# Experts of a small language-model tower: VectorE's small operations dealt out one by one, `up` moved behind `down`, side work moved to other steps

## Chip, cores and metric

One core of a Trainium2 chip. The time is device microseconds of the whole program; the kernel before takes 2905.35 us (median of 3 runs, 2901.58 to 2911.56).

## What is computed

4096 tokens of width 192 pass through an embedding with a block-wise quantisation, an attention layer of 12 heads, and a layer of experts. Only the last is touched:

```python
z = jnp.einsum('nd,sdr->nsr', xf, P)            # xf: layer norm of h; 8 sets, 16 numbers each
scores = jnp.einsum('nsr,smr->nsm', z, C)       # 64 experts in each set
topv, topi = jax.lax.top_k(scores, K)           # K = 4
w = jax.nn.softmax(topv, axis=-1)
h = jax.nn.gelu(jnp.einsum('nsr,nskrh->nskh', z, W1g) + b1g)   # 32 hidden units
yl = jnp.einsum('nskh,nskhr->nskr', h, W2g) + b2g
comb = jnp.einsum('nskr,nsk->nsr', yl, w).reshape(n, S * R)
out = jax.nn.gelu(comb @ G1 + g1b) @ G2 + g2b   # h + out is the result
```

## The kernel before

The experts' stage (`stage_experts`) computes all 64 experts of each set for all tokens, and multiplies the hidden values by a weight that is zero for those not chosen. Tokens go in 8 groups of 512 (NG, GTOK). A group has 32 steps (NSTEP), each with four blocks of 128 hidden rows. A block's way: `up` (L1340) multiplies z by W1 into one of the four PSUM banks 0 to 3; ScalarE's `gelu` (L1483) takes two banks (a pair, 0 or 1) at once into `hid`; `spread_weights` (L1353) copies the block's weights over its rows into one of three ring banks; VectorE's mixture, `mix` (L1609, recorded at L1615), multiplies the two into `hw`; `down` (L1360) adds four blocks by W2 into bank 7, four matrix products on four column groups, in two recorded passes each. `up` reads 50 rows of one half of the array's rows, `spread` 64; z and the weights lie so that each `up` stands on the other half than the `spread` beside it.

TensorE's order in step n is written out by hand: `spread` 2 of step n, the first `up` of pair 1 for step n+1, `down` of step n-1, `spread` 3, the second `up` of that pair, `spread` 0 of step n+1, the first `up` of pair 0 for n+2, `spread` 1, the second `up`; then side items. Each engine runs its own list in order. The first `up` of a pair waits for the GELU that reads its banks (L1342); `down` for the four mixtures of its step.

The three ring banks (`order`, `at`, `ring_bank`, `bank_free`) are dealt out in one list over all `spread` and side items: an item waits until the third one before it has been read. `sides` names the side items of each step: `OUT_AT` the way out of the group before (mixture of sets, GELU, product, `take_out` on VectorE in steps 3 and 4, then GpSimd adds the input in `add_input` and SP stores); `PREP_AT` the scores of the next group (items 3 to 6, two banks at a time) and the turnings of its weights (items 7 to 10); `Z_AT` the turnings of x and `make_z` (items 0 to 2) for the group after the next.

VectorE's own small work for later groups stands between mixtures, in bursts: `normalise` (layer norm) behind the second mixture of steps 7, 13 and 15, `prepare` (maxima, marks, denominators, `keep_marked`, `high_weights`) behind the fourth of steps 14 to 25, `split_z` behind step 22. Eight maxima or marks make a burst. On GpSimd `weights` (L1267) runs `below_best`, `divide` for both halves and then `low_weights` for both halves; `turn_w` (L1329) waits for `low_weights` of its half. ScalarE computes `exponentials` behind step 18.

z goes through HBM and back (`bounce_z`, L1194). SP's list per group g is: `bounce_z(g + 1)`, wait for the output of group g, store it. `score` (L1316) waits for z (`z_in`).

Of the kernel before, what the change touches and what calls it, by code (L numbers as in the profile page):

```python
# [15 lines left out]
ALU = mybir.AluOpType  # L16
# [7 lines left out]
GT = 4  # L24
NG = NT // GT
# [5 lines left out]
S, R, M, HID = 8, 16, 64, 32  # L31
NJ = M * HID // P
NQ = 4
# [902 lines left out]
def stage_experts(nc, f_p, f_c, f_w1, f_b1, f_w2, f_b2, f_g1, f_g1b, f_g2, f_g2b,  # L936
# [15 lines left out]
    TAKEN = -3.0e38  # L952
    NSTEP = 2 * NJ
# [5 lines left out]
    with ExitStack() as own:  # L959
# [26 lines left out]
        side_full, side_free, out_taken = sem("side_full"), sem("side_free"), sem("out_taken")  # L986
# [10 lines left out]
        def work(n):  # L997


            pair, jj = divmod(n, NJ)  # L1000
            return [(2 * pair + i // 2 + NQ * (i % 2), (jj + NJ // 2 * (i % 2)) % NJ) for i in range(4)]
# [140 lines left out]

        Z_AT = {16: (0,), 17: (1,), 20: (2,)}
        PREP_AT = {12: (3, 4), 14: (5, 6), 26: (7,), 27: (8,), 28: (9,), 29: (10,)}
        OUT_AT = {1: (0,), 2: (1,), 3: (2,)}
        EXP_AT = 18
        SPLIT_AT = 22
        BIAS_AT = (18, 21)  # L1150

        def sides(g, n):
            found = [("out", g - 1, k) for k in OUT_AT.get(n, ())] if g else []
# [28 lines left out]
        def ring_bank(item):  # L1182
            return psum[FIRST + at[item] % RING]
# [36 lines left out]
        def _(pool):  # L1220
# [22 lines left out]

            def divide(g, part):
                half = slice(part * GT * S // 2, (part + 1) * GT * S // 2)
                pool.wait_ge(marked, 2 * g + part + 1)
                pool.tensor_tensor(ew[:, half, :], ew[:, half, :],
                                   rden[:, 1, half].unsqueeze(2).to_broadcast([P, GT * S // 2, M]), ALU.mult)\
                    .then_inc(w_scaled, 1)
# [37 lines left out]
        def _(pe):  # L1287
# [49 lines left out]
                                            ident16[:, :])  # L1337
                last.then_inc(side_full, 1)

            def up(g, n, pair, which):  # L1340
                if which == 0:
                    need(pe, gelu_done, g * (2 * NSTEP) + 2 * n - 1 + pair)  # L1342

                low_rows = work(n)[2 * pair][1] < NJ // 2
                i = 2 * pair + (which + 1 if low_rows else which) % 2
                s, j = work(n)[i]
                rows = slice(HALF * (s // NQ), HALF * (s // NQ) + KR)
                last = pe.matmul(psum[i], w1[rows, s % NQ, j * P:(j + 1) * P], zst[rows, g % 2, s % NQ, :],  # L1348
                                 start=True, stop=True)
                if which:  # L1350
                    last.then_inc(up_done, 1)
# [56 lines left out]
            for item in FIRST_ITEMS:  # L1408
                side(*item)
            pe.wait_ge(w_copied, 4)  # L1410
            for n, pair in ((0, 0), (0, 1), (1, 0)):
                up(0, n, pair, 0)
                up(0, n, pair, 1)
            for i in (0, 1):
                spread_weights(0, 0, i)
            for g in range(NG):
                for n in range(NSTEP):
                    next1, next2 = after(g, n), after(g, n, 2)
                    last1 = after(g, n, -1)
                    spread_weights(g, n, 2)  # L1420
                    if next1[0] < NG:
                        up(*next1, 1, 0)
                    if g or n:
                        down(*last1)
                    spread_weights(g, n, 3)
                    if next1[0] < NG:
                        up(*next1, 1, 1)
                        if next1[1] == 0:
                            pe.wait_ge(w_copied, next1[0] * 4 + 4)
                        spread_weights(*next1, 0)  # L1430
                    if next2[0] < NG:
                        up(*next2, 0, 0)
                    if next1[0] < NG:
                        spread_weights(*next1, 1)
                    if next2[0] < NG:
                        up(*next2, 0, 1)
                    if n in BIAS_AT:
                        bias_down(g, BIAS_AT.index(n))
                    for item in sides(g, n):
                        side(*item)  # L1440
# [96 lines left out]
        def _(dve):  # L1537
# [20 lines left out]
            def refine(g):  # L1558
                dve.wait_ge(pow_done, g + 1)
                link(dve.tensor_tensor(newton, rstd, rstd, ALU.mult))  # L1560
                link(dve.tensor_tensor(newton, newton, var, ALU.mult))
                link(dve.tensor_scalar(newton, newton, -0.5, 1.5, ALU.mult, ALU.add))
                dve.tensor_tensor(rstd, rstd, newton, ALU.mult).then_inc(rstd_ready, 1)

            def split_z(g):
                dve.wait_ge(zh_done, g + 1)
                dve.wait_ge(side_free, freed_at["prep", g, 2])
                dve.tensor_tensor(zp[:, 1, :], zc[:, :], zp[:, 0, :].bitcast(F32), ALU.subtract)\  # L1568
                   .then_inc(z_split, 1)

            def top_four(g, k):
                t2, half = divmod(k, 2)
                dve.wait_ge(side_free, freed_at["prep", g, 3 + k])
                dve.memset(holder[:, k:k + 1], 0.0)
                for t in (2 * t2, 2 * t2 + 1):
                    for q in range(NQ):
                        i = (half * NQ + q) * GT + t
                        last = dve.max(top[:, i, :], sc[:, i, :])  # L1578
                if k == 3:
                    link(last)  # L1580

            def denominators(g):
# [1 line left out]
                                  top[:, :, TOPK:TOPK + 1].to_broadcast([P, GT * S, TOPK]), ALU.subtract)\  # L1584
                   .then_inc(den_asked, 1)

            def mark(g, part):
                for i in range(part * GT * S // 4, (part + 1) * GT * S // 4):
                    last = dve.match_replace(scr[:, i, :], top[:, i, :], sc[:, i, :], TAKEN)  # L1589
                if part == 3:  # L1590
                    link(last)

            def reciprocals(g):
# [2 lines left out]
                link(dve.reciprocal(rden[:, 1, :], rden[:, 0, :]))  # L1596

            def keep_marked(g, part):
                half = slice(part * GT * S // 2, (part + 1) * GT * S // 2)
                dve.scalar_tensor_tensor(ew[:, half, :], scr[:, half, 0:M], TAKEN, ew[:, half, :],  # L1600
                                         ALU.is_equal, ALU.mult).then_inc(marked, 1)

            def high_weights(g, part):
                half = slice(part * GT * S // 2, (part + 1) * GT * S // 2)
                by_half = ew[:, half, :].rearrange("p i (h m) -> p i h m", h=2)
                dve.wait_ge(w_scaled, 2 * g + part + 1)
                dve.tensor_copy(wsp[:, half, :, 0, :], by_half).then_inc(w_cast, 1)

            def mix(g, n, blocks):  # L1609
                if (g or n > 1) and 0 in blocks:  # L1610
                    dve.wait_ge(down_done, g * NSTEP + n - 1)
                for q in blocks:
                    dve.wait_ge(gelu_done, g * (2 * NSTEP) + 2 * n + q // 2 + 1)
                    dve.wait_ge(spread, g * (NQ * NSTEP) + NQ * n + q + 1)
                    dve.tensor_tensor(hw[:, n % 2, q, :], hid[:, n % 2, q, :], ring_bank(("w", g, n, q)),  # L1615
                                      ALU.mult).then_inc(mixed, 1)

            def take_out(g, k):
                if k == 0:
# [2 lines left out]
                dve.tensor_tensor(tok(o[:, :])[:, 2 * k:2 * k + 2, :],  # L1622
                                  ring_bank(("out", g, 1 + k)).rearrange("p (t n) -> p t n", t=2)[:, :, 0:D],
                                  g2b_bc[:, :].unsqueeze(1).to_broadcast([P, 2, D]), ALU.add).then_inc(out_taken, 1)
            def prepare(g, n):

                if 14 <= n < 18:
                    top_four(g, n - 14)
                if n == 17:
                    denominators(g)  # L1630
                if 18 <= n < 22:
                    mark(g, n - 18)
                if n == 22:
                    reciprocals(g)
                if n in (22, 23):
                    keep_marked(g, n - 22)
                if n in (24, 25):
                    high_weights(g, n - 24)

            def normalise(g, n):  # L1640

                if n == 7:
                    sums(g)
                if n == 13:
                    variance(g)
                if n == 15:
                    refine(g)

            for g in range(2):
                for n in range(NSTEP):  # L1650
                    normalise(g, n)
                split_z(g)
            for n in range(NSTEP):
                prepare(0, n)
            for g in range(NG):
                for n in range(NSTEP):
                    mix(g, n, (0, 1))
                    if g and n in (3, 4):
                        take_out(g - 1, n - 3)
                    if g < NG - 2:  # L1660
                        normalise(g + 2, n)
                    mix(g, n, (2, 3))
                    if g < NG - 1:
                        prepare(g + 1, n)
                    if n == SPLIT_AT and g < NG - 2:
                        split_z(g + 2)
            for k in range(2):
                take_out(NG - 1, k)

# [24 lines left out]
```

## Time and profile before

| | |
|---|---|
| median of 3 runs | 2905.35 us |
| the profiled execution | 2918.95 us, its span 2917.2 us |
| TensorE busy (matmul) | 2477.4 us, 85% |
| VectorE busy | 1895.8 us, 65% |
| ScalarE busy | 1200.4 us, 41% |
| GpSimd busy | 1155.5 us, 40% |
| mixtures, L1615 | 1024 of 683 ns |
| `up`, L1348; `spread`, L1358 | 1024 of 582 and of 421 ns |
| `down`, L1366 | 2048 records of 664 ns |

The experts run in the last third, from 1950 to the end. A view of the timeline gives for each line its start, its length, the engine, the source line, what it writes and reads, how many merged instructions, and in brackets how long the engine was idle before it and who released it. Matmuls on different parts of the array overlap, so their lengths don't add up. The granted clock is TensorE's, as a share of 2.4 GHz.

### The profile page before, as it was taken

How to read it: one execution, taken by the hardware profiler on the slowest of the kernel's cores; microseconds unless marked ns; L12 is line 12 of the kernel's file. 1: busy time of each engine (PE TensorE's matmuls, PEld its weight loads, DVE VectorE, ACT ScalarE, POOL GpSimd, SP SyncE). 2: the span in 40 equal slices, each digit the busy share in tenths (PEclk: the TensorE clock that was granted, in tenths of full speed). 3: DMA queues.
4: the chain of work that ended last, by engine and by line, in shares of the span. 5: the costliest groups of instructions: out<-in, count | busy, mean ns of one | idle time of the engine just before them, and what ended most of it. 6: DMA issues, size and time to landing. Idle time of an engine off the chain costs nothing. (4 is left out here: it accounts for less than half of the span.)

```text
span 2917.2 us, 42124 instructions
## 1 busy us (share of the span) xinstructions
PE 2477.4 (85%) x16000; PEld 1240.8 (43%) x16000; DVE 1895.8 (65%) x3858; ACT 1200.4 (41%) x1617; POOL 1155.5 (40%) x781
## 2 busy tenths in 40 slices
PE   3556999999999999999999996048888888888898
PEld 1223555565555556555555653022323323232232
DVE  5865565565655656565555654147878888788786
ACT  3421333333333333333333332035656666566565
POOL 5000475666757566575756654021120111201010
PEclk9788999999999999999999998558989999798899
DMA  1002000000010000000000002810101011010100
GB/s 45 11 22 55 7 1 9 1 9 9 1 30 1 9 1 9 9 1 9 1 2 1 3 1 10 72 36 1 24 1 24 1 24 24 1 24 1 24 6 6
DMA packets 78699, 38.51 MB, mean 13 GB/s; under 512 B 62937, under 2 KB 71193, under 8 KB 77849
## 3 DMA queue, kind: packets, MB, share of 16 engines
q1 hardware_dynamic: 76320, 30.98, 6.2%
q10 hardware_dynamic: 640, 1.69, 0.5%
q0 software_dynamic: 1536, 3.15, 0.4%
q8 instruction: 127, 2.08, 0.3%
q14 instruction: 76, 0.61, 0.1%
HBM read 21.93 MB, written 10.49 MB: 11 GB/s over the span
## 5 line engine op out<-in xcount | busy, mean ns | idle before, releaser
L588 POOL TENSOR_TENSOR acc<-acc,pT 128x1024 f32<-128x1024 f32 (+3 forms) x412 | 830.0, 2015 | 243.7 <-ACT pT L907 210.4
L1615 DVE TENSOR_TENSOR hw<-hid,banks 128x512 f32<-128x512 f32 x1024 | 645.7, 683 | 192.0 <-PE banks L1358 187.3
L907 ACT ACTIVATE pT<-banks 128x1024 f32<-128x1024 f32 x480 | 405.7, 896 | 831.1 <-PE banks L661 818.2
L787 DVE TENSOR_REDUCE part<-banks 128x2 f32<-128x1024 f32 (+3 forms) x432 | 438.3, 1044 | 311.7 <-PE banks L637 310.0
L1487 ACT ACTIVATE hid<-banks 128x1024 f32<-128x1024 f32 x512 | 499.5, 1022 | 333.3 <-PE banks L1348 314.7
L1348 PE MATMUL banks<-zst,w1c 50*128 50x512 f32 x1024 | 425.9, 582 | 29.2 <-ACT hid L1487 23.3
L1358 PE MATMUL banks<-wT,select 64*128 64x512 f16 x1024 | 357.5, 421 | 61.6 <-DVE hw L1615 56.9
L677 PE MATMUL banks<-pT,v 128*64 128x512 f32 (+3 forms) x1920 | 404.7, 542 | 1.5 <-POOL pT L576 1.5
L1366 PE MATMUL banks<-hw,w 128*32 128x512 f32 x2048 | 302.0, 664 | 1.4 <-DVE hw L1615 0.8
L1358 PEld LDWEIGHTS banks<-wT,select 64*128 64x128 f16 x1024 | 98.9, 98 | 439.9 <-DVE hw L1615 355.7
L637 PE MATMUL banks<-kh,qh 64*128 64x512 f32 (+1 forms) x960 | 191.1, 393 | 14.5 <-ACT pT L907 5.6
L677 PEld LDWEIGHTS banks<-pT,v 128*64 128x64 f32 x1920 | 116.6, 136 | 202.9 <-issue 180.1
L1348 PEld LDWEIGHTS banks<-zst,w1c 50*128 50x128 f32 x1024 | 169.5, 206 | 76.3 <-ACT hid L1487 68.7
L657 PE MATMUL banks<-shift_rows,ones 64*128 64x512 f32 x960 | 198.9, 411 | 0.2 <-DVE part L787 0.2
L637 PE MATMUL banks<-kl,qh 64*128 64x512 f32 (+1 forms) x960 | 176.3, 362 | 0.0
L637 PE MATMUL banks<-kh,ql 64*128 64x512 f32 (+1 forms) x960 | 176.2, 362 | 0.0
L576 POOL TENSOR_SCALAR_AFFINE_SELECT pT<-pT 128x256 f32<-128x256 f32 x192 | 78.1, 407 | 247.0 <-ACT pT L907 246.8
L661 PE MATMUL banks<-qh,kh 64*128 64x512 f32 x960 | 175.8, 362 | 0.0
L661 PE MATMUL banks<-ql,kh 64*128 64x512 f32 x960 | 175.3, 361 | 0.0
L661 PE MATMUL banks<-qh,kl 64*128 64x512 f32 x960 | 175.3, 361 | 0.0
L657 PEld LDWEIGHTS banks<-shift_rows,ones 64*128 64x128 f32 x960 | 89.8, 183 | 194.8 <-issue 131.2
L830 DVE RECIPROCAL total<-total 128x256 f32<-128x256 f32 x96 | 167.6, 1746 | 3.1 <-ACT total L915 2.7
(183 smaller groups left out, 2901.0 us busy)
## 6 DMA issues: line engine op xcount, KB each, us to landing
zst<-z_scratch SPq DMA_DIRECT2D x48, 128.0 KB, 4.4
z_scratch<-zp SPq DMA_DIRECT2D x8, 512.0 KB, 3.5
out_h<-o SPq DMA_DIRECT2D x8, 384.0 KB, 2.7
xT_scratch<-xs_hi SPq DMA_DIRECT2D x4, 512.0 KB, 2.7
xt_hi<-xT_scratch SPq DMA_DIRECT2D x2, 1024.0 KB, 5.6
w1c<-raw1p ACTq DMA_DIRECT2D x12, 132.0 KB, 4.6
w1c<-raw1p SPq DMA_DIRECT2D x12, 132.0 KB, 4.1
wo<-in_L_attn_W_O SPq DMA_DIRECT2D x12, 96.0 KB, 1.9
```

What stands on the lines that cost most here:

```text
L588: pool.tensor_tensor(acc[:, G % 2, :, off:CH], acc[:, G % 2, :, off:CH], pT[:, slot, :, 0:w], ALU.add).then_inc(summed, 1)
L637: last = pe.matmul(banks[h][:, 0:w], a[head(h), u, i * P:(i + 1) * P], b[head(h), u, c * CH:c * CH + w], start=(k == 0), stop=(k == 2))
L657: pe.matmul(banks[h][:, 0:w], ones[head(h), :], rows[head(h), u, Q, off:CH], start=True, stop=False)
L661: last = pe.matmul(banks[h][:, 0:w], a[head(h), u, kt * P:(kt + 1) * P], b[head(h), u, t0:t0 + w], start=False, stop=(k == 2))
L677: last = pe.matmul(psum[6 + G % 2][head(h), off:CH], v[:, u, kt, head(h)], pT[:, J % PSLOTS, h, 0:CH - off], start=(kt == 0), stop=(j == L ...
L787: last = dve.tensor_reduce(to[:, :, c:c + 1], both[:, :, 0:whole], AX.X, ALU.max)
L907: act.activation(pT[:, J % PSLOTS, :, 0:CH - off], both[:, :, 0:CH - off], ACT.Exp, scale=E ** -0.5)\
L1348: last = pe.matmul(psum[i], w1[rows, s % NQ, j * P:(j + 1) * P], zst[rows, g % 2, s % NQ, :], start=True, stop=True)
L1358: pe.matmul(bank, select[rows, jr, :], wT[rows, g % 2, s, :], start=True, stop=True).then_inc(spread, 1)
L1366: last = pe.matmul(psum[Y][32 * i:32 * i + 32, :], w2[:, s, j, :], hw[:, n % 2, i, :], start=(n == 0), stop=(n == NSTEP - 1))
L1487: act.activation(hid[:, n % 2, 2 * pair:2 * pair + 2, :], banks[:, pair * 1024:(pair + 1) * 1024].rearrange("p (q n) -> p q n", n=GTOK), A ...
L1615: dve.tensor_tensor(hw[:, n % 2, q, :], hid[:, n % 2, q, :], ring_bank(("w", g, n, q)), ALU.mult).then_inc(mixed, 1)
```

## The change

Everything is in the experts' stage. The arithmetic is the same.

- VectorE: one maximum behind each mixture of steps 8 to 15, one mark behind each of steps 16 to 23. `keep_marked` goes in quarters instead of halves (behind the third mixtures of steps 20 and 21, the first and the third of 24), `high_weights` behind the second mixtures of 23 and 26, denominators at 16, reciprocals at 20, sums, variance and refine behind the first mixtures of 5, 7 and 9, `split_z` behind the last of 15. `divide` waits for two quarters. A mark's or a maximum's last one still has VectorE wait for its end, now also at each eighth mark.
- TensorE: `spread` 2, `down`, `spread` 3, first `up` of pair 1, `spread` 0, second `up`, `spread` 1, then both `up` of pair 0. The pair's first product is chosen to lie on the other half of the rows than the `spread` before it.
- Side work: `Z_AT` from 16, 17, 20 to 11, 12, 13; the scores from 12 and 14 to 5 and 7; the turnings of the weights from 26 to 29 to 24, 25, 27, 28; exponentials from 18 to 17; biases from (18, 21) to (18, 22). SP's and GpSimd's lists stay.

```diff
-        Z_AT = {16: (0,), 17: (1,), 20: (2,)}
-        PREP_AT = {12: (3, 4), 14: (5, 6), 26: (7,), 27: (8,), 28: (9,), 29: (10,)}
+        Z_AT = {11: (0,), 12: (1,), 13: (2,)}
+        PREP_AT = {5: (3, 4), 7: (5, 6), 24: (7,), 25: (8,), 27: (9,), 28: (10,)}
         OUT_AT = {1: (0,), 2: (1,), 3: (2,)}
-        EXP_AT = 18
-        SPLIT_AT = 22
-        BIAS_AT = (18, 21)
+        EXP_AT = 17
+        BIAS_AT = (18, 22)
+        BEST_FROM, MARK_FROM = 8, 16
+        KEEP_AT = {(20, 2): 0, (21, 2): 1, (24, 0): 2, (24, 2): 3}
+        HIGH_AT = {(23, 1): 0, (26, 1): 1}
+        DEN_AT, RECIPROCALS_AT = (16, 0), (20, 0)
+        SUMS_AT, VARIANCE_AT, REFINE_AT, SPLIT_AT = (5, 0), (7, 0), (9, 0), (15, 3)
+        TAKE_OUT_AT = {(3, 1): 0, (4, 1): 1}
...
-                pool.wait_ge(marked, 2 * g + part + 1)
+                pool.wait_ge(marked, 4 * g + 2 * part + 2)
...
-            def up(g, n, pair, which):
+            def up(g, n, pair, which, beside=None):
                 if which == 0:
                     need(pe, gelu_done, g * (2 * NSTEP) + 2 * n - 1 + pair)
-
-                low_rows = work(n)[2 * pair][1] < NJ // 2
-                i = 2 * pair + (which + 1 if low_rows else which) % 2
+                    first_of[pair] = 2 * pair
+                    if beside is not None:
+                        gw, nw, iw = beside
+                        first_of[pair] += work(nw)[iw][1] < NJ // 2
+                i = first_of[pair] if which == 0 else 4 * pair + 1 - first_of[pair]
...
                     spread_weights(g, n, 2)
-                    if next1[0] < NG:
-                        up(*next1, 1, 0)
                     if g or n:
                         down(*last1)
                     spread_weights(g, n, 3)
                     if next1[0] < NG:
-                        up(*next1, 1, 1)
+                        up(*next1, 1, 0, (g, n, 3))
                         if next1[1] == 0:
                             pe.wait_ge(w_copied, next1[0] * 4 + 4)
                         spread_weights(*next1, 0)
-                    if next2[0] < NG:
-                        up(*next2, 0, 0)
-                    if next1[0] < NG:
+                        up(*next1, 1, 1)
                         spread_weights(*next1, 1)
                     if next2[0] < NG:
+                        up(*next2, 0, 0, (*next1, 1))
                         up(*next2, 0, 1)
...
-            def mark(g, part):
-                for i in range(part * GT * S // 4, (part + 1) * GT * S // 4):
-                    last = dve.match_replace(scr[:, i, :], top[:, i, :], sc[:, i, :], TAKEN)
-                if part == 3:
+            def mark(g, i):
+                last = dve.match_replace(scr[:, i, :], top[:, i, :], sc[:, i, :], TAKEN)
+                if i % (GT * S // 4) == GT * S // 4 - 1:
                     link(last)
...
             for g in range(NG):
-                for n in range(NSTEP):
-                    mix(g, n, (0, 1))
-                    if g and n in (3, 4):
-                        take_out(g - 1, n - 3)
+                for n, q in GAPS:
+                    mix(g, n, q)
+                    if g and (n, q) in TAKE_OUT_AT:
+                        take_out(g - 1, TAKE_OUT_AT[n, q])
                     if g < NG - 2:
-                        normalise(g + 2, n)
-                    mix(g, n, (2, 3))
+                        normalise(g + 2, n, q)
                     if g < NG - 1:
-                        prepare(g + 1, n)
-                    if n == SPLIT_AT and g < NG - 2:
-                        split_z(g + 2)
+                        choose(g + 1, n, q)
```

## Rows read from the trace of the kernel before

**Rows 1.** Busy time in windows (us), mixtures alone, then all engines, clock, DMA.
```profile
2086.70:2814.50 727.80, 485.26 (x769) 0.91 0.07 15
...
2821.20:2903.30 82.10, 73.28 (x446) 22.76 (x438) 65.79 (x106) 49.68 (x52) 0.00 (x0) 1.00 0.02 6
```

**Rows 2.** Timeline of a plain step: `up`, `down`, `spread`, the fourth mixture, GELUs.
```profile
2231.18 0.49 PE L1348 MATMUL banks<-zst,w1c 50*128 50x512 f32 x1
2231.60 1.07 PE L1366 MATMUL banks<-hw,w 128*32 128x512 f32 x8
...
2232.60 0.39 PE L1358 MATMUL banks<-wT,select 64*128 64x512 f16 x1
2232.60 0.61 PE L1348 MATMUL banks<-zst,w1c 50*128 50x512 f32 x2
...
2233.09 2.48 DVE L1615 TENSOR_TENSOR hw<-hid,banks 128x512 f32<-128x512 f32 x4 [0.60 <-PE banks L1358]
2233.20 1.94 ACT L1487 ACTIVATE hid<-banks 128x1024 f32<-128x1024 f32 x2 [1.15 <-PE banks L1348]
```

**Rows 3.** Group 2 by windows, mixtures alone: VectorE busy, clock, DMA share, GB/s.
```profile
2197.70:2211.10 13.40, 10.09 (x16) 1.00 0.01 2
2211.10:2220.60 9.50, 7.53 (x12) 1.00 0.29 102
2220.60:2233.05 12.45, 9.93 (x16) 1.00 0.44 61
2233.05:2294.50 61.45, 35.67 (x56) 0.87 0.00 1
2294.50:2316.90 22.40, 17.73 (x29) 0.97 0.00 1
```

**Rows 4.** Timeline of the last step: `spread` 2 with no `up` beside it, `down`.
```profile
2900.78 0.39 PE L1358 MATMUL banks<-wT,select 64*128 64x512 f16 x1 [0.51 <-DVE hw L1615]
2901.09 1.06 PE L1366 MATMUL banks<-hw,w 128*32 128x512 f32 x8
```

**Rows 5.** Timeline, VectorE: maxima in a burst; a mark.
```profile
2247.29 0.99 DVE L1578 MAX8 top<-sc 128x8 f32<-128x68 f32 x7
...
2267.11 0.21 DVE L1589 MATCH_REPLACE8 scr<-top,sc 128x68 f32<-128x68 f32 x1
```

**Rows 6.** Timeline, TensorE: scores; the first half of `make_z` at the full clock.
```profile
2240.66 1.08 PE L1325 MATMUL banks<-w1c,zst 48*128 48x64 f32 x16 [0.93 <-DVE hw L1615]
...
2518.07 1.13 PE L1313 MATMUL banks<-x2t_hi,pm_hi 128*128 128x512 f32 x2
```

**Rows 7.** Timeline in group 2: `take_out`, SP's issues; line L1204's landing.
```profile
2212.93 0.55 DVE L1622 TENSOR_TENSOR o<-banks,g2b_bc 128x384 f32<-128x384 f32 x1
...
2215.90 0.45 SPq L1198 DMA_DIRECT2D z_scratch<-zp  x1
2219.47 2.66 SPq L1204 DMA_DIRECT2D zst<-z_scratch  x6
...
DMA to landing us min/median/max: 2.9/4.4/5.8
```

**Rows 8.** Timeline, GpSimd: a half divided, a half's low parts.
```profile
2292.89 1.90 POOL L1247 TENSOR_TENSOR ew<-ew,rden 128x1024 f32<-128x1024 f32 x1 [1.84 <-DVE ew L1600]
...
2299.09 2.14 POOL L1255 TENSOR_TENSOR wsp<-ew,wsp 128x1024 f16<-128x1024 f32 x1 [1.05 <-DVE wsp L1607]
```

**Rows 9.** Timeline, ScalarE: first table load for the exponentials; GELUs after.
```profile
2268.56 1.28 ACT L1473 ACT_TABLE_LOAD   x1
...
2273.28 1.94 ACT L1487 ACTIVATE hid<-banks 128x1024 f32<-128x1024 f32 x2
```

**Rows 10.** Windows of group 2, all engines: an idle TensorE; the slow stretch behind.
```profile
2247.00:2249.00 2.00, 0.00 (x0) 0.01 (x1) 2.00 (x12) 1.57 (x2) 0.00 (x0) 1.00 0.00 0
...
2251.50:2258.30 6.80, 6.80 (x28) 2.54 (x25) 4.84 (x21) 3.07 (x4) 0.18 (x1) 0.50 0.01 2
```

**Rows 11.** Timeline, TensorE: `down` in that slow stretch.
```profile
2254.42 1.94 PE L1366 MATMUL banks<-hw,w 128*32 128x512 f32 x8
```

More of the change, by code:

```diff
@@ L1410, in _ @@
             pe.wait_ge(w_copied, 4)
+            first_of = [0, 0]
             for n, pair in ((0, 0), (0, 1), (1, 0)):
@@ L1569, in split_z, with best @@
                    .then_inc(z_split, 1)
-            def top_four(g, k):
+            def best(g, m):
+                k, r = divmod(m, GT * S // 4)
                 t2, half = divmod(k, 2)
[L1573 to L1579, printed above, removed]
+                if r == 0:
+                    dve.wait_ge(side_free, freed_at["prep", g, 3 + k])
+                    dve.memset(holder[:, k:k + 1], 0.0)
+                i = (half * NQ + r % NQ) * GT + 2 * t2 + r // NQ
+                last = dve.max(top[:, i, :], sc[:, i, :])
+                if m == GT * S - 1:
                     link(last)
@@ L1598, in keep_marked @@
             def keep_marked(g, part):
-                half = slice(part * GT * S // 2, (part + 1) * GT * S // 2)
-                dve.scalar_tensor_tensor(ew[:, half, :], scr[:, half, 0:M], TAKEN, ew[:, half, :],
+                quarter = slice(part * GT * S // 4, (part + 1) * GT * S // 4)
+                dve.scalar_tensor_tensor(ew[:, quarter, :], scr[:, quarter, 0:M], TAKEN, ew[:, quarter, :],
                                          ALU.is_equal, ALU.mult).then_inc(marked, 1)
@@ L1607, in high_weights, with mix @@
                 dve.tensor_copy(wsp[:, half, :, 0, :], by_half).then_inc(w_cast, 1)
-            def mix(g, n, blocks):
-                if (g or n > 1) and 0 in blocks:
+            def mix(g, n, q):
+                if (g or n > 1) and q == 0:
                     dve.wait_ge(down_done, g * NSTEP + n - 1)
[L1612 to L1616, printed above, removed]
+                dve.wait_ge(gelu_done, g * (2 * NSTEP) + 2 * n + q // 2 + 1)
+                dve.wait_ge(spread, g * (NQ * NSTEP) + NQ * n + q + 1)
+                dve.tensor_tensor(hw[:, n % 2, q, :], hid[:, n % 2, q, :], ring_bank(("w", g, n, q)),
+                                  ALU.mult).then_inc(mixed, 1)
             def take_out(g, k):
@@ L1624, in take_out, with choose @@
                                   g2b_bc[:, :].unsqueeze(1).to_broadcast([P, 2, D]), ALU.add).then_inc(out_taken, 1)
[L1625 to L1629, printed above, removed]
+            def choose(g, n, q):
+                if BEST_FROM <= n < BEST_FROM + 8:
+                    best(g, (n - BEST_FROM) * NQ + q)
+                if (n, q) == DEN_AT:
                     denominators(g)
-                if 18 <= n < 22:
-                    mark(g, n - 18)
-                if n == 22:
+                if MARK_FROM <= n < MARK_FROM + 8:
+                    mark(g, (n - MARK_FROM) * NQ + q)
+                if (n, q) == RECIPROCALS_AT:
@@ L1634, in prepare, with normalise @@
                     reciprocals(g)
[L1635 to L1642, printed above, removed]
+                if (n, q) in KEEP_AT:
+                    keep_marked(g, KEEP_AT[n, q])
+                if (n, q) in HIGH_AT:
+                    high_weights(g, HIGH_AT[n, q])
+            def normalise(g, n, q):
+                if (n, q) == SUMS_AT:
@@ L1643, in normalise @@
                     sums(g)
-                if n == 13:
+                if (n, q) == VARIANCE_AT:
                     variance(g)
-                if n == 15:
+                if (n, q) == REFINE_AT:
                     refine(g)
+                if (n, q) == SPLIT_AT:
+                    split_z(g)
+            GAPS = [(n, q) for n in range(NSTEP) for q in range(NQ)]
             for g in range(2):
-                for n in range(NSTEP):
-                    normalise(g, n)
-                split_z(g)
@@ L1653, in _ @@
-            for n in range(NSTEP):
-                prepare(0, n)
+                for n, q in GAPS:
+                    normalise(g, n, q)
+            for n, q in GAPS:
+                choose(0, n, q)
             for g in range(NG):
-                for n in range(NSTEP):
-                    mix(g, n, (0, 1))
-                    if g and n in (3, 4):
-                        take_out(g - 1, n - 3)
+                for n, q in GAPS:
+                    mix(g, n, q)
+                    if g and (n, q) in TAKE_OUT_AT:
+                        take_out(g - 1, TAKE_OUT_AT[n, q])
```

## Prediction

> **What bounds the kernel now.** The diff touches only the experts, so I read that stage. The windows of its mixtures give the frame: six middle groups last 727.8 us, 121.3 each, and in the last group 82.1 us go by at the full clock with nothing but plain steps [rows 1]. A plain step is the thing to understand first. Its timeline [rows 2] shows TensorE held by a loop that runs through ScalarE: `up` of pair 1 starts at 2231.18, just as a GELU has ended; `down` behind it at 2231.60; the next `spread` and the pair's second `up` at 2232.60; the GELU of that pair at 2233.20, 1.02 long; and the next first `up` after it: 0.42 + 1.00 + 0.60 + 1.02 + 0.05 = 3.09 us. VectorE's four mixtures take 2.48 and it then idles 0.60 before the fourth. So a plain step is not bound by an engine but by where `up` stands: ahead of `down`.
>
> The second reading is by stretches of group 2, cut at the start of a step's fourth mixture [rows 3]. Steps 0 to 3 last 13.4, 4 to 6 9.5, 7 to 10 12.4 (12.5 to the start itself), 11 to 24 61.4, 25 to 31 22.4. Fourteen plain steps would be 43.3: steps 11 to 24 lose 18 us to bursts on VectorE, to side work on TensorE, to the exponentials, and to a clock granted at 0.87 there.
>
> **The plain step after.** `down` now stands behind `spread` 2 alone, and both `up` of pair 1 behind `spread` 3, so the GELU's loop is no longer than 0.3 + 0.6 + 1.02 + 0.05 = 2.0. What is late next is a loop through VectorE: the fourth mixture ends, `spread` 2 and `down` wait for it; `down` starts 0.32 behind that `spread` [rows 4], the third `spread` (bank 3) 1.00 later, its mixture 0.49 later and lasts 0.69 [rows 2]; with 0.05 for the first release that is 2.55. Four mixtures alone are 4 x 0.60 = 2.40, under it. The `up` and `spread` behind `down` go in pairs on the two halves of the rows as before, so they fit. Plain: 3.09 to 2.55.
>
> **VectorE's operations, singly.** Seven maxima in a row span 0.99, some 0.13 each by starts, and a mark lasts 0.21, its load beside it [rows 5]. One in each gap gives steps of 4 x (0.60 + 0.14) = 2.97 with maxima, and 4 x (0.60 + 0.21) = 3.24 with marks; both above 2.55, so VectorE sets them, and TensorE's wait for a burst goes. No row shows one such operation between mixtures. Nothing overlapping at all would add 0.08 each (0.21 a maximum, 0.29 a mark with its load), 5 us a group; below nothing isn't possible. I take the pitch in the burst, the nearest row.
>
> **Side work.** A side item sits between `spread` 1 and `spread` 2 of the next step, and takes its bank from the fourth mixture, so it adds itself to the loop: scores about 1.0 and they also wait one mixture more (step 4.1), `make_z` two halves of 1.1 (step 4.7) [rows 6], turnings of x and w 0.6 (3.3 and 3.15). Before, part of this lay beside VectorE's bursts.
>
> **The scores' move is what costs.** Scores of group g+1 go from steps 12 and 14 to 5 and 7, while the transfers they need stay. SP bounces z(g+1) through HBM only after the store of group g-1's output, which hangs on `take_out` in step 4. In group 2: `take_out` starts 2212.93, z_scratch is written at 2215.90, the six loads of zst are issued from 2219.47 for 2.7 us, each lands 2.9 to 5.8 later, 4.4 in the middle [rows 7]. The last issue is at about 2221.7, so z is in at 2224.6 to 2227.5, 11.7 to 14.6 behind `take_out`; the last of six that queue on one another is nearer to the slow end, and I take 14. Today the scores run at 2240.66 [rows 6], 13 us after z; then nobody sees it. After the change, `take_out` starts 1.8 behind the fourth mixture of step 3, so z is in at 15.8; TensorE would reach the scores at 3.3 + 3.5 + 0.7 = 7.5. It stands for 8.3 us, all `spread`, `down` and `up` queued behind it, and VectorE after two more mixtures. That holds for the bounces of groups 2 to 7, so in groups 1 to 6.
>
> **A second wait, at the turnings.** `turn_w` starts at step 24 instead of 26, but the last two quarters of `keep_marked` are in step 24 too. GpSimd divides the second half (1.90) and only then writes the first half's low parts (2.14) [rows 8], for which the turning waits. From the fourth mixture of step 24: 0.15 + 1.90 + 2.14 + 0.1 = 4.3, then 0.5 of turning, 0.3, 1.0 and 0.5 to the next fourth mixture: step 25 takes 6.6 instead of 3.15.
>
> **The exponentials.** ScalarE is away from GELUs from 2268.56 to 2273.28, 4.7 us with both table loads [rows 9]. Moved to 17, they start 4.2 into that step; the GELU for step 19's third mixture ends 9.9 behind its start, and steps of 3.3 would want it at 8.2: 1.8 lost, less than today, since `down` and `spread` 3 no longer queue behind the `up` that waits for this GELU. The table loads remain. Split z, sums, variance and refine only move: nothing is hidden that wasn't.
>
> **The clock.** Where TensorE ran nothing from 2247.0 to 2249.0, a stretch granted 0.50 (1.2 GHz) follows from 2251.5 to 2258.3 [rows 10], and `down` spans 1.94 there instead of 1.06 [rows 11]. Stalls of 8 and of 4 us should bring that too. At this level the scores take about 1.7, `spread` to `down` 0.6, `down` 1.87, the release 0.71. The Trainium skill, TensorE: Matmul & The Clock Gate, section "What's actually happening", says the same from the other side: the throttled state is the default, and activity releases it. By that rule each stall here ends at 1.2 GHz and the sum is the one below; with the full clock held through the stalls it would be the first rival's.
>
> **The sum for a middle group**, in stretches as in rows 3:
> - steps 0 to 3: 2.6 + 2.6 + 3.5 + 3.3 = 12.0 for 13.4: -1.4
> - 4 to 6: the scores start at 15.9, then 1.7 + 0.6 + 1.87 + 0.71 = 20.8 for 9.5: +11.3
> - 7 to 10: 3.9 (still slow) + 4.1 + 3.7 (refine, 0.8) + 3.0 = 14.7 for 12.5: +2.2
> - 11 to 24: 3.0 + 3.3 + 3.3 + 4.7 + 3.0 + 4.2 (split, denominators) + 3.2 + 3.3 + 5.0 (exponentials) + 4.7 (reciprocals, a quarter) + 3.8 + 3.3 + 3.8 + 3.9 = 52.5, and 1.4 for 8 us at half clock; 53.9 for 61.4: -7.5
> - 25 to 31: 6.6 + 3.15 + 2.55 + 3.15 + 3.15 + 2.55 + 2.55 = 23.7, and 2.0 of half clock behind the stall; 25.7 for 22.4: +3.3
>
> That is +7.9 for group 2, whose 119.2 is 2.1 under the mean of 121.3: +5.8 on the mean, times six +35. The first group (I take it as long as the others) has no wait for z (its steps 4 to 6 take 2.6 + 3.5 + 4.1, +0.7 in place of +11.3), and a fast step 7, 0.5 less: together 5.8 - 10.6 - 0.5, some -5, and -6 with its four first steps, which lose 0.5 each but have no way out to shorten. The last has none of this work: 27 plain steps gain 0.54 each, and its first four 1.4: -16. Ahead of the stage, `reciprocals` waits in the midst of the marks and the low parts come later: +2. Sum 35 - 6 - 16 + 2 = +15. The profiled execution lasts 2918.95 (span 2917.2), 0.5% over the median of 2905.35; I carry the difference over: 2920, slower by 0.5%.
>
> **Rivals.**
> - The clock stays at 2.4 GHz, or comes back at once. The 61.4 us at 0.87 speak against it; the long plain stretch at 1.00 [rows 1], and steps less idle than today's, for it. It takes back 2.6 (scores and step 7), 1.4 and 2.0 a group: 6.0 x 6 + 3.4 = 40. 2880, faster. This is the other side: the same stalls, decided by whether a stall's end is slow; below some 3 us of clock loss a group the change is even.
> - z is in before the scores. That needs a transfer 8 us quicker than in any group; only a chain I misread would do it. It gives back 10.4 x 6 = 63: 2857.
> - The order on TensorE brings nothing: the plain step stays at 3.09, as some other release (a pair not running beside the other, `spread` 1 late) closes a loop. Some five plain steps in each middle group, eight in the first, 29 in the last, 0.54 each, 36 in all: 2956. Rows 2 speak against it: the pairs start together.
>
> **Numbers.** Forecast 0.55 (by itself 2895 to 2945: z at 11.7 or 14.6 gives -14 to +4, the clock 15 either way, single operations up to 36 if nothing overlapped); clock kept 0.22; z in time 0.06; no gain from the order 0.17. Range 2870 to 2958. About 0.3%, 9 us, can be told from no change. The forecast's own spread leaves 0.42 slower, 0.11 within, 0.02 faster; with the rivals: slower 0.59, the same 0.13, faster 0.28.
>
> **What would show it.** Right: a wait of TensorE for zst of about 8 us in groups 1 to 6 and none in group 0; a plain step of 2.55 in the last group, whose 82 us fall to some 68 over the same steps; steps 8 to 23 at 3.0 and 3.2 with no burst of maxima; a wait of 3 to 4 us for GpSimd ahead of the first turning; ScalarE's table loads with a wait of 1.8 behind them. Wrong: no DMA among TensorE's releasers; a plain step at 3.09; a granted clock of 1.00 behind the stalls.

## The result, and the profile after

The changed kernel takes 2927.44 us (median of 4 runs, 2926.17 to 2933.74) beside 2906.17 for the kernel before: a ratio of 1.0077, interval 1.0054 to 1.0100. It is slower by 0.8%; the forecast was 2920 from 2905, slower by 0.5%. The page of its profile:

```profile
span 2924.8 us, 42167 instructions
...
PE 2440.8 (83%) x16000; PEld 1233.9 (42%) x16000; DVE 1894.8 (65%) x3874; ACT 1199.3 (41%) x1617; POOL 1151.3 (39%) x781
...
PEclk9778999999999999999999998559899998999999
```

VectorE is as busy as before (1894.8 and 1895.8 us) and TensorE 37 us less, so the added time is in waits. The stretches of rows 3, in group 2 of the changed kernel (mixtures alone: VectorE busy, granted clock, DMA share, GB/s):

```profile
2196.70:2209.65 12.95, 10.09 (x16) 1.00 0.01 2
2209.65:2230.30 20.65, 7.61 (x12) 0.77 0.37 83
2230.30:2244.50 14.20, 10.55 (x16) 0.98 0.00 1
2244.50:2296.20 51.70, 37.78 (x56) 0.97 0.00 1
2296.20:2322.70 26.50, 17.92 (x29) 0.87 0.00 1
```

Against [rows 3]: steps 0 to 3 gain 0.5 us, 4 to 6 lose 11.2, 7 to 10 lose 1.8, 11 to 24 gain 9.8, 25 to 31 lose 4.1. The long stretch in the middle gained what the change was made for, and two short ones, where the mean clock was 0.77 and 0.87, lost more than that. The releasers in the experts' stage (who waited for whom: us, times, longest) name the two, and neither is in the profile of before:

```profile
PE banks L1332 <- DMA zst<-z_scratch: 52.0, 6, 10.1
...
PE banks L1343 <- POOL wsp L1262: 28.9, 7, 4.1
```

L1332 is the scores and L1343 the first turning of the weights (L1325 and L1336 before). TensorE's timeline in group 2 shows the first of them and what follows it, SP's the reason:

```profile
2216.55 0.61 PE L1358 MATMUL banks<-zst,w1c 50*128 50x512 f32 x2
2225.46 1.92 PE L1332 MATMUL banks<-w1c,zst 48*128 48x64 f32 x16 [8.29 <-DMA zst<-z_scratch]
2227.16 0.63 PE L1368 MATMUL banks<-wT,select 64*128 64x512 f16 x1
2227.73 1.08 PE L1376 MATMUL banks<-hw,w 128*32 128x512 f32 x4
```

```profile
2213.94 0.39 SPq L1221 DMA_DIRECT2D out_h<-o  x1
2214.43 0.45 SPq L1205 DMA_DIRECT2D z_scratch<-zp  x1
2217.98 2.66 SPq L1211 DMA_DIRECT2D zst<-z_scratch  x6
```

`take_out` starts at 2211.45, SP's issues follow as in [rows 7], and the scores begin 14.0 us behind it. The second wait, GpSimd and then TensorE in step 25:

```profile
2296.39 1.90 POOL L1254 TENSOR_TENSOR ew<-ew,rden 128x1024 f32<-128x1024 f32 x1 [9.19 <-DVE ew L1608]
2298.25 2.12 POOL L1262 TENSOR_TENSOR wsp<-ew,wsp 128x1024 f16<-128x1024 f32 x1
```

```profile
2300.52 1.01 PE L1343 MATMUL banks<-ident,wsp 128*128 128x128 f16 x8 [4.13 <-POOL wsp L1262]
2301.47 0.61 PE L1368 MATMUL banks<-wT,select 64*128 64x512 f16 x1
2302.00 1.93 PE L1376 MATMUL banks<-hw,w 128*32 128x512 f32 x8
```

`down` spans 1.93 here, where [rows 11] have 1.94. The windows of the two stretches (all engines; the column 0.50 is the granted clock, 1.2 GHz) each begin inside a wait, at 2220.6 and at 2299.1:

```profile
2220.60:2230.70 10.10, 5.24 (x32) 2.88 (x32) 1.09 (x2) 1.09 (x2) 0.00 (x0) 0.50 0.34 44
2299.10:2305.90 6.80, 5.38 (x27) 2.18 (x28) 2.01 (x4) 1.68 (x2) 1.27 (x1) 0.50 0.00 0
```

The plain step, in the last group: from one `spread` 2 to the next it is 2.56 us by these rows and 2.55 in nearly all steps, where [rows 2] led to 3.09. `down` starts 0.32 behind `spread` 2, `spread` 3 0.99 behind `down`, and all four `up` stand behind it, in pairs with a `spread`.

```profile
2880.14 0.39 PE L1368 MATMUL banks<-wT,select 64*128 64x512 f16 x1 [0.15 <-DVE hw L1622]
...
2880.46 1.07 PE L1376 MATMUL banks<-hw,w 128*32 128x512 f32 x8
...
2881.45 0.39 PE L1368 MATMUL banks<-wT,select 64*128 64x512 f16 x1
...
2882.70 0.39 PE L1368 MATMUL banks<-wT,select 64*128 64x512 f16 x1
```

### The profile page after: what moved, and what is told of

It is laid out like the page before. It is cut to its first block and busy times, and to the rows that moved or that the text cites. A ratio compares the mean times of both kernels' runs of the same rounds, so it can differ in the third digit from the quotient of the medians.

```text
span 2924.8 us, 42167 instructions
## 1 busy us (share of the span) xinstructions
PE 2440.8 (83%) x16000; PEld 1233.9 (42%) x16000; DVE 1894.8 (65%) x3874; ACT 1199.3 (41%) x1617; POOL 1151.3 (39%) x781
## 3 DMA queue, kind: packets, MB, share of 16 engines
q0 software_dynamic: 1536, 3.15, 0.4%
## 5 line engine op out<-in xcount | busy, mean ns | idle before, releaser
L1622 DVE TENSOR_TENSOR hw<-hid,banks 128x512 f32<-128x512 f32 x1024 | 666.8, 679 | 196.6 <-PE banks L1368 177.7
L1368 PE MATMUL banks<-wT,select 64*128 64x512 f16 x1024 | 369.7, 409 | 60.9 <-DVE hw L1622 43.1
L1358 PE MATMUL banks<-zst,w1c 50*128 50x512 f32 x1024 | 340.0, 566 | 11.2 <-ACT hid L1495 9.8
L1376 PE MATMUL banks<-hw,w 128*32 128x512 f32 x2048 | 293.9, 648 | 7.1 <-DVE hw L1622 7.1
L1358 PEld LDWEIGHTS banks<-zst,w1c 50*128 50x128 f32 x1024 | 142.8, 201 | 17.5 <-ACT hid L1495 12.6
```

The lines of the kernel that those rows point to most:

```text
L1368: pe.matmul(bank, select[rows, jr, :], wT[rows, g % 2, s, :], start=True, stop=True).then_inc(spread, 1)
L1376: last = pe.matmul(psum[Y][32 * i:32 * i + 32, :], w2[:, s, j, :], hw[:, n % 2, i, :], start=(n == 0), stop=(n == NSTEP - 1))
```

## Experiments

Windows of an experiment are of group 2, mixtures alone, cut at the start of a fourth mixture as above, unless said otherwise. A single step's length is counted from its first mixture to the next step's first.

**The kernel before once more.** No edit.

> The kernel before, unchanged, once more with its profile. The medians differ by 21 us (2906.2 and 2927.4), the two profiled spans by only 7.6 (2917.2 and 2924.8). Theory A: the profiled execution of before was a slow one of its own kind, because the half-clock stretches in steps 11 to 24 fall differently from run to run (61.3 to 65.8 us for the same steps in its groups, against 51.6 to 52.2 after); then this profile gives another span, between 2902 and 2917, with other lengths for steps 11 to 24, while steps 0 to 10 repeat within 0.1 us. Rival: the profiler itself costs before 13 us and the changed kernel nothing; then the span is 2917 again, with the same lengths.

Median 2908.84, ratio to the kernel before 0.9998 (0.9984 to 1.0012); the profiled span is 2905.0. The stretches of group 2:

```profile
2195.60:2209.10 13.50, 10.13 (x17) 1.00 0.01 2
2209.10:2218.50 9.40, 7.47 (x12) 1.00 0.29 100
...
2231.00:2292.60 61.60, 35.75 (x57) 0.87 0.00 1
```

The short stretches repeat. The mixtures' stage lasts 941 us, where the profile that the prediction was made from had 951: in groups 4 to 6 steps 11 to 31 were 11 us longer there, with more half clock (166 us in all against 149). So theory A holds, and the loss is seen in full only from this profile: the stage goes from 941 to 956, and its first mixture from 1949.8 to 1955.9. Of these 6.1 us 1.9 lie between the denominators and the first mixture; the rest lies ahead of them, in code that the change doesn't touch and whose end falls between 1923.8 and 1934.2 in the runs below.

**z ahead of the store.**

```diff
-                if 1 <= g < NG - 1:
-                    bounce_z(g + 1, (g + 1) % 2)
+                if g < NG - 2:
+                    bounce_z(g + 2, g % 2)
                 sp.wait_ge(out_ready, g + 1)
```

> The changed kernel, but SP bounces z of group g+2 ahead of its wait for the output of group g, so z is in at the end of a group and not 14 us behind take_out. Nothing else differs. Theory A (the scores wait for z): steps 4 to 6 of groups 1 to 6 fall from 20.9 to 3.3 + 3.5 + 4.1 = 10.9 us, no wait of TensorE for zst is left, and the time falls by 6 x 10 = 60 us, to about 2867. Rival (the scores at steps 5 and 7 cost by their own length, by ring banks and by a slow clock, and z is only the last releaser named): the steps stay above 15 us and the time above 2895.

2873.37 us, ratio 0.9889 (0.9868 to 0.9909): 54 us less than the changed kernel, 60 expected; the rival gave at most 32. No releaser named zst is left. In groups 4 and 5 steps 4 to 6 take 10.8 us, as added up, but in groups 1 and 2 13.0: there the clock falls to half at the scores of step 5 without a stall. In group 2 it falls at 2210.1, as the scores start, and TensorE had been idle for at most 0.63 us at a time in the ten microseconds before:

```profile
2201.95:2214.94 12.99, 7.61 (x13) 0.81 0.09 31
```

```profile
2210.09 1.92 PE L1332 MATMUL banks<-w1c,zst 48*128 48x64 f32 x16 [0.63 <-DVE hw L1622]
```

The wait for z is shown. The two profiled spans differ by 57 us. Steps 4 to 6 of the six groups took 3 us more than added up and steps 11 to 24 another 3 more than in the changed kernel, both in groups with more half clock; that the missing microseconds are clock is read from this and not tested by itself.

**Low parts ahead of the second division.**

```diff
                 divide(g, 0)
-                divide(g, 1)
                 low_weights(g, 0)
+                divide(g, 1)
                 low_weights(g, 1)
```

> The changed kernel, but GpSimd writes the first half's low parts ahead of the second half's division, so the first turning no longer waits for that division. Theory A: step 25 falls from 8.41 us to about 3.3, 5 us in each of seven groups, and some 2 us ahead of the stage: 36 us less, about 2891. Rival (the wait moves on: the second half's low parts come later and hold the third turning at step 27, or the slow clock stays): step 25 falls but steps 26 to 29 grow by 2 or more, and the time falls by less than 20.

2899.25 us, ratio 0.9959 (0.9940 to 0.9978): 28 us less, 36 expected; the rival gave under 20. Step 25 falls from 8.41 to 3.15, and 26 to 31 don't grow:

```profile
2293.00:2296.10 3.10, 2.48 (x4) 1.00 0.00 0
2296.10:2313.80 17.70, 15.38 (x25) 1.00 0.01 1
```

The 2 us ahead of the stage were not got back (27.6 from the denominators to the first mixture, 27.8 in the changed kernel, 26.0 before), and in groups 1 to 5 steps 7 to 10 took 14.2 to 16.3 instead of 14.1 to 14.6. Over all groups steps 25 to 31 gained 40 us, and steps 7 to 24 lost 12 of them again, where the half clock grew from 42 to 93 us.

**Both.** The two edits together.

> Both edits together: SP bounces z ahead of its wait for the output, and GpSimd writes the first half's low parts ahead of the second division. Theory A (two independent waits): the gains add, 60 + 36 = 96 us less than the changed kernel, about 2831, so 2.6% faster than the kernel before; a middle group takes 126 - 10 - 5 = 111 us. Rival (both gains draw on the same slow clock, or VectorE's work becomes the limit): less than 80 us in all, above 2847.

2828.52 us, ratio 0.9730 (0.9713 to 0.9747): 99 us less than the changed kernel, 96 expected, and more than the 82 of the two alone. By the profiles the stage is 53 us shorter with the first edit, 28 with the second and 92 with both, so 10 us of the excess over the two alone lie in the stage; the rest lies ahead of it or between executions. With both waits gone, the stage has 84 us at half clock instead of 166, and steps 7 to 24 have 70 where the second edit alone left 93. Group 2:

```profile
2185.50:2196.30 10.80, 7.58 (x12) 1.00 0.12 37
...
2262.60:2283.40 20.80, 17.85 (x28) 1.00 0.06 16
```

**TensorE's order alone.** The kernel before with `up` and the loop over steps as in the change, nothing else.

> The kernel before with TensorE's new order alone (down behind spread 2, both up of pair 1 behind spread 3, the last up alone). VectorE's bursts, the scores at 12 and 14 and all other places stay. Theory A (the GELU loop set the plain step): plain steps fall from 3.09 to 2.55, the last group from 100.1 to about 87, a middle group by some 7 us (0.5, 1.1, 1.5, 3 and 1 in the five stretches), in all 60 us less than before: about 2848. Rival (the order brings its gain only once VectorE's bursts are gone, as these set the steps): only the last group gains, 13 us, about 2895.

2839.82 us, ratio 0.9755 (0.9715 to 0.9794); 2848 expected. Steps 4 to 6 take 8.4, 7 to 10 11.1, the last group 86.3 us instead of 100.1. In group 2 steps 11 to 24 stay at 61.4, at a clock of 0.82; in the other groups before the last they take 53.4 to 62.0:

```profile
2185.40:2193.80 8.40, 7.52 (x12) 1.00 0.32 109
...
2204.90:2266.30 61.40, 35.54 (x56) 0.82 0.00 1
```

One part of the change, by itself, is 2.5% faster than the kernel before. The rest of the change took that away. The ratio of the whole change without its two waits, 0.9730, is hardly another one (the intervals overlap), so the order is nearly all that shows of what the change brings.

**The old order in the changed kernel.** (The label says that both waits are gone; they are both in this kernel, as the expectation has it.)

> The changed kernel with the old order on TensorE (first up of pair 1 ahead of down); VectorE's single operations and the new places stay, and so do both waits, for z and for the low parts. Theory A: against the changed kernel (2927) plain steps return to 3.09 (five in a middle group, 27 in the last), steps with maxima rise from 2.92 to 3.09, the exponentials hold down and spread 3 back again, 2 us: 5.5 us in a group and 13 in the last, about 51 in all: 2978. Rival (with single operations the order no longer matters, as VectorE sets the steps): only the last group loses, 2940.

2987.59 us, ratio 1.0266 (1.0223 to 1.0309): 60 us over the changed kernel, 51 expected. The order is worth 69 us with VectorE's bursts and 60 without, so it hardly depends on them. Of the 60, step 19 alone is 2.4 us a group (7.49 for 5.08): a first `up` that waits for its GELU behind the exponentials stands ahead of `down` only in the old order. A part of the 60 may be clock: the stage has 247 us of half clock instead of 166, and steps 7 to 10 take 15.3 to 19.0 in the middle groups.

**The scores early, in the kernel before.**

```diff
-        PREP_AT = {12: (3, 4), 14: (5, 6), 26: (7,), 27: (8,), 28: (9,), 29: (10,)}
+        PREP_AT = {5: (3, 4), 7: (5, 6), 26: (7,), 27: (8,), 28: (9,), 29: (10,)}
```

> The kernel before with its scores at steps 5 and 7 and nothing else changed. Theory A (they wait there for z, whatever VectorE and the order on TensorE do): steps 4 to 6 of groups 1 to 6 grow from 9.5 to about 20.5 us, steps 11 to 24 get back some 3 us as the scores leave the bursts: 6 x 8 = 48 us more, about 2957. Rival (the wait came from the faster steps of the changed kernel alone, which reach the scores sooner): under 20 us more, below 2929.

2971.54 us, ratio 1.0205 (1.0160 to 1.0250), so 62 us slower; 48 expected, the rival under 20. Steps 4 to 6 take 21.2:

```profile
2218.70:2239.90 21.20, 7.63 (x13) 0.72 0.37 80
```

TensorE's waits name the same transfer as in the changed kernel:

```profile
PE banks L1325 <- DMA zst<-z_scratch: 56.0, 6, 9.8
```

The move by itself makes the wait. What I had missed is in steps 7 to 10, 13.6 to 17.6 us for 12.5; there is half clock in them (1 to 13 us a group), and none in the kernel before.

**TensorE kept busy in the stall.**

```diff
                 if t2 == 0:
+                    if g > 1:
+                        for _ in range(36):
+                            pe.matmul(banks[0], select[:, 0, :], wT[:, (g - 1) % 2, 0, :], start=True, stop=True)
                     pe.wait_ge(z_in, g * 96 + 96)
```

> The changed kernel with 36 products of 512 columns on the scores' own bank ahead of the wait for z in groups 1 to 6, about 7.8 us at 2.4 GHz, which the scores then overwrite. The wait for z stays as long; only TensorE is busy in it. Theory A (the stall ends at 1.2 GHz and that costs 2 to 3 us on top of the wait): the granted clock stays 1.00 over the scores and steps 4 to 6 take about 18.7 us instead of 20.9, 13 us less in all, about 2914. Rival (the slow clock behind the stall costs nothing, as VectorE or the banks set the steps): the same time within 4 us, 2927.

2924.08 us, ratio 1.0051 (1.0032 to 1.0071): 3 us less, which isn't clear of the noise (2917.5 to 2930.0 beside 2926.2 to 2933.7); 13 were expected, at most 4 by the rival. The rival has the time right but not the reason. Steps 4 to 6 fall to 18.8 to 19.4 in the four groups where the clock stays at 1.00, as theory A has it, but the slow stretch comes later, in group 2 in step 8, behind the second scores, and steps 7 to 10 grow by 1.6:

```profile
2208.70:2227.50 18.80, 7.63 (x13) 1.00 0.41 92
2227.50:2243.30 15.80, 10.52 (x17) 0.78 0.00 1
```

Over all groups steps 4 to 6 gain 10.6 us, 7 to 10 lose 7.8 and 11 to 24 lose 3.1, and the stage lasts 956 us, as in the changed kernel. The half clock falls from 166 to 134 us, yet what is new of it, 32 us, lies in steps 7 to 24, where TensorE works. So this run moved the slow clock, and its price stayed about the same.

**Order and dealing, no places moved.** The run with the order alone, and VectorE's maxima and marks two behind each mixture of their old steps:

```diff
-                for t in (2 * t2, 2 * t2 + 1):
-                    for q in range(NQ):
-                        i = (half * NQ + q) * GT + t
-                        last = dve.max(top[:, i, :], sc[:, i, :])
+                t = 2 * t2 + gap // 2
+                for q in (2 * (gap % 2), 2 * (gap % 2) + 1):
+                    i = (half * NQ + q) * GT + t
+                    last = dve.max(top[:, i, :], sc[:, i, :])
```

> The kernel before with two parts of the change and no place moved: TensorE's new order (as in the run with that alone), and VectorE's maxima and marks dealt out two behind each mixture of the same steps as before (14 to 17 and 18 to 21) instead of eight at the end of each. Theory A (a burst costs because TensorE's ring banks, down and the GELUs run dry behind it, and the clock with them): steps 14 to 17 take about 3.4, 4.1, 3.4 and 3.7 us, 18 to 21 about 4.0, 4.0, 5 and 5; steps 11 to 24 fall from some 59.5 to 53, in all 45 us less than with the order alone (2840): about 2795. Rival (what a burst costs is VectorE's own time, which stays the same): steps 11 to 24 stay above 57 and the time above 2825.

2828.90 us, ratio 0.9709 (0.9681 to 0.9737): 11 us less than the order alone by the medians, 45 expected. By the stage it is 19 (876 to 857 us); this profile's stage began late, at 1960. In group 2 steps 16 to 19 take 3.44, 3.8, 4.0 and 4.0, near what was added up. The steps behind side work don't. The rival's time, above 2825, is met, but its reason isn't: steps 11 to 24 are 2.8 us a group shorter than with the order alone, and under 57 in four of the seven groups. Step 21, in which `make_z` lies on the loop, is a clean pair, since the same program does the same in groups 2 and 3, at two clocks (all engines, clock 0.56 and 1.00):

```profile
2249.45:2257.08 7.63, 7.33 (x21) 1.78 (x20) 4.15 (x22) 2.90 (x4) 0.00 (x0) 0.56 0.01 2
2361.33:2365.88 4.55, 4.25 (x22) 1.34 (x22) 4.16 (x22) 2.90 (x4) 0.00 (x0) 1.00 0.00 0
```

The slow clock costs 3.1 us there. VectorE's work is the same in both, 4.15 and 4.16 us.

**`make_z` beside a step that is long on VectorE.**

```diff
-        Z_AT = {16: (0,), 17: (1,), 20: (2,)}
+        Z_AT = {16: (0,), 17: (1,), 21: (2,)}
-        SPLIT_AT = 22
-        BIAS_AT = (18, 21)
+        SPLIT_AT = 23
+        BIAS_AT = (18, 20)
```

> The order and the dealing of the run before (2829), with make_z one step later, at 21, the second biases at 20 and split_z at 23. In step 22 VectorE has the reciprocals and half of keep_marked, 4.8 us of its own, so make_z (2.2 us at the full clock) should lie beside it, where at step 20 it lies on the loop of step 21, 4.55 us at the full clock and 7.6 at half. Theory A: step 21 falls to about 4.0 and step 22 stays within 0.5 of 4.8; at a mean of 2.2 us in six groups, 13 us less: about 2816. Rival (the slow stretch comes with any long product and goes along with make_z, so that step 22 is the one to grow to 7 or more): the same time within 4 us, 2829.

2813.77 us, ratio 0.9664 (0.9638 to 0.9690): 15 us less, 13 expected. Steps 11 to 24 take 53.8 us in group 2, which was 56.2. Cut at the fourth mixture, what was 7.63 is 4.24, at a clock of 0.64, and the step after it 4.59:

```profile
2235.31:2239.55 4.24, 4.24 (x29) 1.08 (x28) 4.07 (x22) 1.81 (x2) 0.00 (x0) 0.64 0.00 0
2239.55:2244.14 4.59, 4.59 (x25) 1.64 (x24) 3.06 (x8) 3.02 (x4) 0.00 (x0) 0.96 0.02 4
```

This is the fastest of the versions: 3.4% faster than the kernel before. The expectation had step 22 within 0.5 us of 4.8; counted from first mixture to first mixture it is 5.9, so a part of `make_z` is still to be seen, and what the move gains in group 2 is the sum of the two steps, 8.8 against 10.9. In group 3 of the run before, at the full clock, the two took 7.6, against 8.5 in group 3 here. So the move gains nothing where the clock was full; what goes with its gain is the half clock in the stage, which falls from 102 to 64 us.

## Why the prediction was right, step by step

The mechanism was right: two waits that weren't there before, a shorter plain step, a half clock at the end of each wait. The size of the sum is partly luck, as the last item says.

- **The plain step.** 2.55 predicted and measured. The new binding loop, fourth mixture, `spread` 2, `down`, `spread` 3, is the one that was named; the pairs on the two halves of the rows cost nothing more. The third rival falls.
- **Single operations.** Steps with maxima alone take 2.92 (2.97 predicted), with marks alone 3.19 to 3.30 (3.24). A mixture starts 0.73 behind the one before with a maximum in between, so the maximum costs 0.13, its pitch in the burst.

```profile
2243.07 0.67 DVE L1622 TENSOR_TENSOR hw<-hid,banks 128x512 f32<-128x512 f32 x1
2243.65 0.22 DVE L1587 MAX8 top<-sc 128x8 f32<-128x68 f32 x1
2243.80 0.67 DVE L1622 TENSOR_TENSOR hw<-hid,banks 128x512 f32<-128x512 f32 x1
```

- **The wait for z.** 8.3 us predicted, 8.29 in group 2; steps 4 to 6 20.8 predicted, 20.4 to 21.4 in the six groups. It is absent in group 0. The second rival falls, and two runs (z sooner, scores early alone) show the cause from both sides.
- **The wait at the turning.** Step 25 was put at 6.6 and 2.0 of clock for it and its neighbours; it took 8.41 in every group, and steps 25 to 31 take 26.4 on a mean against 25.7.
- **The exponentials.** 5.0 predicted for step 19, 5.08 measured. VectorE's longest wait for a GELU is 1.7 us, where 1.8 was forecast.
- **The clock.** The slow stretches came in both stalls, at 0.50, and the first rival falls. That agrees with the rule cited from the Trainium skill, TensorE: Matmul & The Clock Gate. What the slow clock costs in the stalls fits the stretch times (20.65 for 20.8) but no run shows it by itself: the filler run moved the slow clock and won nothing clear, so the 40 us that the first rival gave for a full clock aren't shown either. The pair of steps in the last run but one shows a price, 3.1 us, in another place.
- **What was off.** Steps 0 to 3 were put at 12.0 and took 12.9. The term that failed is step 1, 2.6 for 3.51: `down` of step 0 waits until ScalarE has copied the group before out of bank 7 (0.59 long), and that copy stands behind a GELU. Before, the slower step hid most of it; in the changed kernel TensorE waits. The profile names VectorE as the releaser, but by the kernel's code this `down` also waits for the copy, which ends at 2201.17, 0.14 ahead of it; no run takes the copy away.

```profile
2200.03 0.39 PE L1368 MATMUL banks<-wT,select 64*128 64x512 f16 x1
2200.58 0.59 ACT L1501 ACTIVATE comb<-banks 128x512 f32<-128x512 f32 x1
...
2201.31 1.07 PE L1376 MATMUL banks<-hw,w 128*32 128x512 f32 x8 [0.89 <-DVE hw L1622]
```

  Against it, steps 11 to 24 were put at 53.9 and took 51.7: the 1.4 for half clock were hardly needed (3.4 us of it in most groups, in the stretch 2282.1 to 2285.5 in group 2), and `make_z` cost 4.34 for 4.7. The last group gained 13 for 16: the same step 1 (0.9), step 4, which stayed at 3.29 and was counted as plain (0.5), two steps of 3.1 (1.1), and two of 2.9 (0.5). The first gained 7.5 for 6 against the first profile (122.7 to 115.2), though its steps 4 to 6 took 11.5 for 10.2, and the stretch from the denominators to the first mixture lost 1.9 for 2.
- **The sum.** +15 was forecast on the profiled execution. From that very execution the profiled span grew by 7.6 only, since it was a long one; from the second profile of the kernel before it grew by 19.8, and the medians by 21. A middle group takes 125.6 us on a mean, where it took 121.3 in the first profile and 119.5 in the second: +4.3 and +6.1 for +5.8 forecast. Part of that match is luck, errors that cancel: in group 2 the forecast has 0.9 too little in steps 0 to 3 and 0.7 too little in 25 to 31, 0.5 too much in 7 to 10 and 2.2 too much in 11 to 24.

## What to carry to other kernels

Before a consumer is moved earlier, find who issues its transfer and what stands ahead of that issue in the same queue: the scores were moved seven steps forward while their DMA stayed behind the previous group's output, and some 8 us of stall a group, with the second wait behind it, ate the gain that TensorE's new order brings by itself. In a hand-ordered loop, look for the chain that returns to its own start, add it up from one step's timeline, and then add up the next one; both sums held to 0.01 us here. Where side work on this chain meets a slow clock, try it beside a step that another engine makes long: here that gained 15 us, and nothing in the group that had the full clock already.

## What the runs showed of the hardware

- The price of a stall on TensorE isn't local. It waits 52.0 us for z and 28.9 at the turnings, in all groups together; the stage became 53 us shorter without the first wait, 28 without the second and 92 without both (medians of the whole: 54, 28 and 99). The half-clock time in the stage was 166 us with both, 133 and 164 with one of them gone, 84 with neither.
- 36 products of 512 columns in a stall kept the clock at 2.4 GHz through it in four of six groups, and the fall to 1.2 GHz came at 2233.1 in group 2, where the changed kernel had it at 2220.6; the stage didn't become shorter.
- The clock fell to 1.2 GHz without a stall too: at 2210.1 in the run with z ahead of the store, behind ten microseconds in which TensorE was never idle for more than 0.63 us at a time.
- A change from GELU to exponential on ScalarE took 1.28 us for the load, and the next activation began 0.01 to 0.02 us behind it, in both directions (2268.56 and 2271.99 before, 2270.17 and 2273.59 after).
- Two executions of the kernel before differ by 12 us (spans of 2917.2 and 2905.0). Of these, 9 lie in the experts' stage, where the longer one has 16 us more half clock. A sum against one profile needs a second one to be read to 0.3%.
